# Causal attention with a block FFN: the key tiles of a query block in another order

## The chip, the cores and the metric

The kernel runs on one core of one Trainium2 chip. The metric is the device time of one execution in microseconds (us), lower is better. TensorE (PE) multiplies, VectorE (DVE), ScalarE (ACT) and GpSimd (POOL) do the elementwise work, and SyncE (SP) issues the transfers.

## The reference

Two sequences of 2048 rows with 256 features go through pre-normalised causal attention with 16 heads of 64, a residual and a layer norm, then a gated FFN with a residual and a layer norm:

```python
hn = (h - mu) * rsqrt(var + 1e-05) * gamma + beta
q, k, v = rope(hn @ Wq + bq), rope(hn @ Wk + bk), hn @ Wv + bv      # 16 heads of 64
attn = softmax(where(tril, einsum('bihd,bjhd->bhij', q, k) / 8, -inf))
x = layernorm(h + (einsum('bhij,bjhd->bihd', attn, v) @ Wo + bo + h))
x = layernorm(x + (silu(x @ wg) * (x @ wu)) @ wd)                   # weights are int / 127
```

## The kernel before

After a prologue come 16 iterations, one for each pair of heads and sequence (8 pairs, 2 sequences), and after them the output projection and the FFN. The change lies in the iterations.

**Units.** The 2048 queries are 4 blocks of 512 columns, the keys are 16 tiles of 128. A unit (`UNITS`) is one key tile against one query block, for both heads of the pair. Block b has 4b + 4 key tiles, so an iteration has 4 + 8 + 12 + 16 = 40 units. The last four tiles of a block lie on the diagonal: the unit of tile 4b + i works only on the columns from 128i on, so it is 512, 384, 256 or 128 columns wide, and it has four small matmuls with the mask (L1215) as well. All other units are 512 wide without a mask. I call a unit by its width, with an m where it has the mask: 512, 512m, 384m, 256m, 128m.

**Groups.** Two units in a row are a group; an iteration is 20 groups, g0 to g19. Block 0 is g0 and g1, block 1 g2 to g5, block 2 g6 to g11, block 3 g12 to g19. What PE does in a group is written out by hand, in this order:

1. M1, a piece of the maxima: scores of a later iteration or block in single precision of one part (L1184), written to `m_ps`, of which there is one buffer. DVE reduces it (L833), and no further maxima start before that.
2. S, the scores of the two units into `s_ps` (L1205 to L1215), each behind the exponential of the unit two before.
3. M2, a second piece of maxima (not in g1, g5, g11 and g19, where `M_COUNT` is 1).
4. One use of the bank `x_ps` from the table `XUSE`: T, the turn of the maxima of the next block (L1222, in g1, g5, g11, g19); or X, a piece of the projection of the next pair's q or k, or of v (L1139 to L1141, in g3, g4, g7, g8, g10, g13, g15, g17 for q and k, and g9, g14, g16, g18 for v in most iterations).
5. M3, a third piece, in g3, g8, g13 and g15.
6. W, probabilities times values for the two units of the group before (L1239).
7. R, the row sums of a finished block (L1246), in g0, g2, g6 and g12, behind the last W of that block.

**The other engines.** ACT takes the exponential of each unit (L591) into one of five slots of `pt`. POOL adds the slot into the sums `acc` (L542; the first two units of a block by L537, and in block 0 also L532). R waits until POOL is through with the block. DVE works in its own fixed order: in each group T's input (L847), the transpose of R's result (L882), the rotary products of the X of the group before (L860, L864, which free `x_ps`), the reductions of M1 and M2, the rounding rest of the piece before (L876), the division of a finished block (L887, L890, L895), then the sum with the half that was swapped (L871), which waits for transfers that SP issues behind L860 (`rot<-qr`), and last the reduction of M3.

All this order is static: each engine follows its own list, and semaphores count units, so none of it moves with the key tile that a unit holds.

Of the kernel before, what the change touches and what calls it, by code (L numbers as in the profile page):

```python
# [5 lines left out]
ALU = mybir.AluOpType  # L6
# [7 lines left out]
P = 128  # L14
# [12 lines left out]
BLOCKS = SEQ // NB  # L27
# [4 lines left out]
MASKED = -1e30  # L32


UNITS = [(b, j, max(0, j - 4 * b) * P) for b in range(BLOCKS) for j in range(4 * b + 4)]
NU = len(UNITS)

MUNITS = [(t, c, min(NB, (t + 1) * P - c * NB)) for t in range(TT) for c in range(t // 4 + 1)]
# [14 lines left out]
def units_to(b):  # L53

    return sum(4 * a + 4 for a in range(b))
# [46 lines left out]
def postln_block_kernel(nc, h, gamma, beta, wqkv, bqk, bv, wo, bo, wgate_t, wup_t, wdown_t,  # L102
                        cos, sin, ident, masks, attn, hn_far, v_far, out):
    h, out = h.rearrange("b s d -> (b s) d"), out.rearrange("b s d -> (b s) d")
    with ExitStack() as ctx:
        def sb(name, shape, dt):
            return ctx.enter_context(nc.sbuf_tensor(name, shape, dt))
# [13 lines left out]
        ones_f = sb("ones_f", [P, DK], F32)  # L121
# [20 lines left out]
        with ExitStack() as ctx_attn:  # L142
            def sba(name, shape, dt):
                return ctx_attn.enter_context(nc.sbuf_tensor(name, shape, dt))
# [17 lines left out]
            acc = sba("acc", [P, 2, 2, NB], F32)  # L162
# [144 lines left out]
        FIRST, MIDDLE, SWITCH, LAST = "first", "middle", "switch", "last"  # L307

        def each_pair(engine, pair):

            kinds = {0: FIRST, PAIRS - 1: SWITCH, 2 * PAIRS - 1: LAST}
            for it in range(2 * PAIRS):
                pair(kinds.get(it, MIDDLE), it, it % 2, it % PAIRS, it // PAIRS)
# [3 lines left out]
        def group_units(g):  # L317
            return range(GU * g, GU * g + GU)
# [192 lines left out]
        @block.gpsimd  # L511
        def _(pool):
            pool.wait_ge(primed, 1)

            def next_rows(t):

                nc.gpsimd.tensor_scalar(h_all[1][:, t, :], h_all[1][:, t, :], mv[:, TT + t, 0:1],
                                        rstd[:, TT + t:TT + t + 1], ALU.subtract, ALU.mult).then_inc(next_norm, 1)

            def pair(kind, it, par, pr, batch):  # L520
                for u in range(NU):
                    blk, j, q0 = UNITS[u]
                    if j == 0 and blk > 0:
                        continue
                    pool.wait_ge(exped, it * NU + (u + 1))
                    if j <= 1 and (kind is not FIRST or blk >= 2):
                        pool.wait_ge(r_done, it * BLOCKS + (blk - 1))
                    for a in range(2):
                        sums = acc[:, blk % 2, a, q0:NB]
                        probs = pt[:, u % SLOTS, a, q0:NB]  # L530
                        if j == 0:
                            last = nc.gpsimd.tensor_tensor(acc[:, 0, a, 0:P], probs[:, 0:P],  # L532
                                                           ones_f[:, 0:1].broadcast_to([P, P]), ALU.mult)
                            if a == 1:
                                last.then_inc(summed, 1)
                        elif j == 1:
                            last = nc.gpsimd.tensor_tensor(sums, pt[:, (u - 1) % SLOTS, a, q0:NB], probs, ALU.add)  # L537
                            if a == 1:
                                last.then_inc(summed, 4 if blk > 0 else 3)
                        else:  # L540
                            pool.wait_ge(summed, it * (2 * NU) + (2 * u + a - 1))
                            nc.gpsimd.tensor_tensor(sums, sums, probs, ALU.add).then_inc(summed, 1)  # L542


            pool.wait_ge(a_rstd, len(STAT_TILES))
            for t in range(TT):
                next_rows(t)
            each_pair(pool, pair)

        @block.scalar  # L550
        def _(act):
# [30 lines left out]
            def exp_unit(kind, it, u):  # L582
                blk, j, q0 = UNITS[u]
                if kind is not FIRST or u >= SLOTS:
                    act.wait_ge(pv_done, it * NG + ((u - SLOTS) // GU + 1))
                    act.wait_ge(summed, it * (2 * NU) + 2 * (u - SLOTS + 1))
                if kind is FIRST and u == 0:
                    act.wait_ge(a_turned, 2 * TURNS)
                act.wait_ge(scored, it * NU + (u + 1))
                two = 2 * (u % 2)  # L590
                nc.scalar.activation(pt[:, u % SLOTS, :, q0:NB], s_ps[:, two:two + 2, q0:NB], ACT.Exp, scale=SCALE)\  # L591
                  .then_inc(exped, 1)
# [544 lines left out]
        def _(pe):  # L1137
# [55 lines left out]
            def scores(kind, it, par, u):  # L1193
                blk, j, q0 = UNITS[u]
                if kind is not FIRST or u >= 2:
                    pe.wait_ge(exped, it * NU + (u - 1))
                if j == 0:
                    pe.wait_ge(aux_done, it * BLOCKS + (blk + 1))
                    pe.wait_ge(qk_lo, it * (2 * BLOCKS) + 2 * (blk + 1))
                q, k = slice(NB * blk + q0, NB * (blk + 1)), slice(j * P, (j + 1) * P)  # L1200
                two = 2 * (u % 2)
                dst = [s_ps[:, two + a, q0:NB] for a in range(2)]
                diag = j >= 4 * blk
                for a, rows in enumerate(halves):
                    nc.tensor.matmul(dst[a], qk[par][rows, 1, k], qk[par][rows, 0, q], start=True, stop=False)  # L1205
                for a, rows in enumerate(halves):
                    nc.tensor.matmul(dst[a], qk[par][rows, 1, k], qk[par][rows, 2, q], start=False, stop=False)  # L1207
                for a, rows in enumerate(halves):
                    nc.tensor.matmul(dst[a], qk[par][rows, 3, k], qk[par][rows, 0, q], start=False, stop=False)  # L1209
                for a, rows in enumerate(halves):  # L1210
                    last = nc.tensor.matmul(dst[a], ones_r[rows, :], aux[rows, q0:NB], start=False, stop=not diag)  # L1211
                if diag:
                    for x in range(2):
                        for a, rows in enumerate(halves):
                            last = nc.tensor.matmul(s_ps[:, two + a, q0 + DK * x:q0 + DK * (x + 1)],  # L1215
                                                    mask_b[rows, x, :], id_b[rows, :], start=False, stop=x == 1)
                last.then_inc(scored, 1)
# [7 lines left out]
            def weigh(kind, it, par, g):  # L1225

                for u in group_units(g):
                    blk, j, q0 = UNITS[u]
                    n = 4 * blk + 4
                    pe.wait_ge(exped, it * NU + (u + 1))  # L1230
                    if j == 0:
                        if blk == 0:
                            pe.wait_ge(v_in, 16 * (it + 1))
                        if blk == BLOCKS - 1:
                            pe.wait_ge(v_in3, 16 * (it + 1))
                        if blk > 0 or kind is not FIRST:
                            pe.wait_ge(o_out, it * BLOCKS + blk)
                    for a, rows in enumerate(halves):
                        last = nc.tensor.matmul(o_ps[rows, q0:NB], v[par][:, j, rows], pt[:, u % SLOTS, a, q0:NB],  # L1239
                                                start=(j == 0), stop=(j == n - 1), skip_group_check=True)  # L1240
                last.then_inc(pv_done, 1)

            def sums(it, blk):
# [5 lines left out]
            def pair(kind, it, par, pr, batch):  # L1249
# [30 lines left out]
                for g in range(NG):  # L1280
# [24 lines left out]
                    if g > 0:  # L1305
                        weigh(kind, it, par, g - 1)
                    elif kind is not FIRST:
                        weigh(kind, it - 1, 1 - par, NG - 1)
# [101 lines left out]
            pe.wait_ge(c_lo, OC)  # L1410
            project_out(0, o_first)
            weigh(LAST, FINAL, 1, NG - 1)
            pe.wait_ge(r_turned, FINAL * BLOCKS + 3)
            sums(FINAL, BLOCKS - 1)
# [63 lines left out]
```

## Time and profile before

| | |
|---|---|
| median of 3 runs | 2231.38 us (2230.36 to 2232.55) |
| the profiled execution's own time | 2229.82 us |
| its span in the trace | 2228.0 us |
| PE busy | 2070.0 us, 93% |
| DVE busy | 1597.6 us, 72% |
| POOL busy | 1391.7 us, 62% |
| ACT busy | 906.6 us, 41% |

A share of busy time is an average over the prologue, the iterations and the FFN. The iterations take the time from 72.9 us to about 1880 us. The rows of a timeline give the start and the length of a run of equal instructions, and in brackets the time that the engine stood idle before it and what ended that. Matmuls overlap, so the cost of a step on PE is read from the start of its first matmul to the start of the next step's.

### The profile page before, as it was taken

The page shows a single profiled execution, that of the slowest core. Times are in us where ns is not written, and L with a number is a line of the kernel's source. Part 1 is how long each engine was busy: PE and PEld are TensorE (multiplying, and loading weights), DVE is VectorE, ACT ScalarE, POOL GpSimd, SP SyncE. Part 2 cuts the span into 40 slices and gives each one's busy share as a digit, 9 for nine tenths or more (in the row PEclk, how much of TensorE's full clock was granted, in tenths as well). Part 3 has the DMA queues.
Part 4 walks back from the last instruction along what each step waited for, and adds up shares of the span by engine and source line. Part 5 has one row for each costly group of instructions (what it writes and reads, how often), then busy time and mean ns, then how long its engine had stood idle before and what let it go on. Part 6 is the DMA issues. An engine that isn't in the chain of part 4 may idle for free.

```text
span 2228.0 us, 37497 instructions
## 1 busy us (share of the span) xinstructions
PE 2070.0 (93%) x14720; PEld 1287.2 (58%) x14720; DVE 1597.6 (72%) x2262; ACT 906.6 (41%) x1245; POOL 1391.7 (62%) x1204
## 2 busy tenths in 40 slices
PE   6779999999999989999999999999999989889997
PEld 5445555555555545555555555555555545789996
DVE  8576878686878776767777777778787763556654
ACT  4424443444444434434343434343434345434342
POOL 1457777777787866677767777878787879000000
PEclk9899999999999999999999999999999999999999
DMA  6311212121202122122111212121112131231300
GB/s 223 119 30 38 62 39 62 39 62 39 58 25 68 42 68 72 45 65 63 48 53 43 58 43 58 43 58 34 48 34 58 29 119 48 67 104 57 112 10 29
DMA packets 116149, 132.16 MB, mean 59 GB/s; under 512 B 15248, under 2 KB 71184, under 8 KB 115728
## 3 DMA queue, kind: packets, MB, share of 16 engines
q1 hardware_dynamic: 115984, 129.92, 19.5%
q8 instruction: 109, 1.79, 0.3%
q14 instruction: 56, 0.46, 0.1%
HBM read 56.47 MB, written 39.85 MB: 43 GB/s over the span
## 4 chain that ended last, share of the span: by engine, by line
PE 60%; DVE 24%; DMA 5%; SPq 4%; issue 4%; ACT 1%; POOL 1%; ACTq 0%; DVEq 0%
PE o_ps L1239 13%; DVE mpart L833 9%; PE m_ps L1184 7%; DMA rot<-qr 5%; PE s_ps L1205 4%; SPq L385 4%; PE s_ps L1209 4%; PE s_ps L1207 4%; PE s_ps L1211 4%; PE x_ps L1139 3%; DVE qr L860 3%; PE x_ps L1246 3%; DVE qc L871 2%; PE gu_ps L1139 2%; PE gu_ps L1140 2%
## 5 line engine op out<-in xcount | busy, mean ns | idle before, releaser
L542 POOL TENSOR_TENSOR acc<-acc,pt 128x512 f32<-128x512 f32 (+3 forms) x1024 | 1195.8, 1200 | 228.0 <-ACT pt L591 228.0
L591 ACT ACTIVATE pt<-s_ps 128x1024 f32<-128x1024 f32 (+3 forms) x640 | 544.8, 895 | 704.8 <-PE s_ps L1211 342.4
L833 DVE TENSOR_REDUCE mpart<-m_ps 128x2 f32<-128x1024 f32 (+2 forms) x576 | 624.9, 1085 | 288.2 <-PE m_ps L1184 215.7
L1239 PE MATMUL o_ps<-pt,v 128*64 128x512 f32 (+3 forms) x2560 | 547.5, 549 | 0.0
L1184 PE MATMUL m_ps<-qk 64*128 64x512 f32 (+3 forms) x1280 | 290.0, 449 | 85.0 <-DVE mpart L833 73.7
L1184 PEld LDWEIGHTS m_ps<-qk 64*128 64x128 f32 x1280 | 121.1, 185 | 395.6 <-DVE mpart L833 223.6
L1239 PEld LDWEIGHTS o_ps<-pt,v 128*64 128x64 f32 x2560 | 157.8, 138 | 239.1 <-issue 213.8
L537 POOL TENSOR_TENSOR acc<-pt 128x512 f32<-128x512 f32 (+1 forms) x128 | 161.7, 1283 | 193.7 <-ACT pt L591 193.7
L1205 PE MATMUL s_ps<-qk 64*128 64x512 f32 (+3 forms) x1280 | 253.7, 392 | 0.0
L1209 PE MATMUL s_ps<-qk 64*128 64x512 f32 (+3 forms) x1280 | 235.6, 363 | 0.0
L1211 PE MATMUL s_ps<-aux,ones_r 64*128 64x512 f32 (+3 forms) x1280 | 234.7, 362 | 0.0
L1207 PE MATMUL s_ps<-qk 64*128 64x512 f32 (+3 forms) x1280 | 234.3, 362 | 0.0
L871 DVE TENSOR_TENSOR qc<-qc,rot 128x512 f32<-128x512 f32 x128 | 139.6, 1091 | 113.4 <-DMA rot<-qr 113.3
L569 ACT ACTIVATE qk<-qc 128x512 fp32r<-128x512 f32 x128 | 80.0, 629 | 253.2 <-DVE qc L871 253.2
L876 DVE TENSOR_TENSOR qk<-qc,qk 128x512 fp32r<-128x512 f32 x128 | 140.8, 1103 | 0.2 <-ACT qk L569 0.2
L1209 PEld LDWEIGHTS s_ps<-qk 64*128 64x128 f32 x1280 | 121.2, 185 | 20.3
L1211 PEld LDWEIGHTS s_ps<-aux,ones_r 64*128 64x128 f32 x1280 | 121.5, 185 | 19.1
L1207 PEld LDWEIGHTS s_ps<-qk 64*128 64x128 f32 x1280 | 122.1, 187 | 16.5
L1205 PEld LDWEIGHTS s_ps<-qk 64*128 64x128 f32 x1280 | 122.1, 187 | 15.8 <-ACT pt L591 4.9
L1139 PE MATMUL x_ps<-hn,w_hl 128*128 128x512 f32 x240 | 107.7, 449 | 0.0
L1141 PE MATMUL x_ps<-hn,w_hl 128*128 128x512 f32 x240 | 95.3, 397 | 0.0
L1140 PE MATMUL x_ps<-hn,w_hl 128*128 128x512 f32 x240 | 95.1, 396 | 0.0
(165 smaller groups left out, 2882.0 us busy)
## 6 DMA issues: line engine op xcount, KB each, us to landing
rot<-qr SPq DMA_DIRECT2D x512, 64.0 KB, 2.0
attn<-o_sum SPq DMA_DIRECT2D x64, 256.0 KB, 2.3
o_raw<-attn SPq DMA_DIRECT2D x8, 2048.0 KB, 8.9
v<-v_far SPq DMA_DIRECT2D x16, 768.0 KB, 5.2
v_far<-v_part SPq DMA_DIRECT2D x48, 256.0 KB, 2.0
w_raw<-in_wqkv SPq DMA_DIRECT2D x34, 128.0 KB, 5.1
v_far<-v SPq DMA_DIRECT2D x16, 256.0 KB, 2.4
v<-v_far SPq DMA_DIRECT2D x16, 256.0 KB, 5.0
```

The source lines that it names most:

```text
L537: last = nc.gpsimd.tensor_tensor(sums, pt[:, (u - 1) % SLOTS, a, q0:NB], probs, ALU.add)
L542: nc.gpsimd.tensor_tensor(sums, sums, probs, ALU.add).then_inc(summed, 1)
L591: nc.scalar.activation(pt[:, u % SLOTS, :, q0:NB], s_ps[:, two:two + 2, q0:NB], ACT.Exp, scale=SCALE)\
L833: nc.vector.tensor_reduce(dst, m_ps[:, :, 0:w], AX.X, ALU.max, negate=True).then_inc(maxed, 1)
L871: nc.vector.tensor_tensor(qc[:, c % 2, a, :], qc[:, c % 2, a, :], rot[:, a, :], ALU.add).then_inc(roped, 1)
L1139: nc.tensor.matmul(dst, lhs[0], rhs[0], start=first, stop=False)
L1184: last = nc.tensor.matmul(m_ps[:, a, 0:w], qk[par][rows, 0, q], qk[par][rows, 1, k], start=True, stop=not diag)
L1205: nc.tensor.matmul(dst[a], qk[par][rows, 1, k], qk[par][rows, 0, q], start=True, stop=False)
L1207: nc.tensor.matmul(dst[a], qk[par][rows, 1, k], qk[par][rows, 2, q], start=False, stop=False)
L1209: nc.tensor.matmul(dst[a], qk[par][rows, 3, k], qk[par][rows, 0, q], start=False, stop=False)
L1211: last = nc.tensor.matmul(dst[a], ones_r[rows, :], aux[rows, q0:NB], start=False, stop=not diag)
L1239: last = nc.tensor.matmul(o_ps[rows, q0:NB], v[par][:, j, rows], pt[:, u % SLOTS, a, q0:NB], start=(j == 0), stop=(j == n - 1), skip_group ...
```

## The change

The key tiles of a block come in an order given by a table. Tile 0 stays first. The two units of a group are now:

| block | groups before | groups after |
|---|---|---|
| 0 | g0 512m 384m, g1 256m 128m | g0 512m 256m, g1 384m 128m |
| 1 | g2, g3 whole, g4 512m 384m, g5 256m 128m | g2 whole, g3 512m 384m, g4 512 256m, g5 512 128m |
| 2 | g6 to g9 whole, g10 512m 384m, g11 256m 128m | g6 whole, g7 512 256m, g8 whole, g9 512m 384m, g10 whole, g11 512 128m |
| 3 | g12 to g17 whole, g18 512m 384m, g19 256m 128m | g12, g13 whole, g14 512 256m, g15, g16 whole, g17 512m 384m, g18 whole, g19 512 128m |

(whole: 512 and 512.) What each group does besides its two units is as before, and so are all waits, which count units. The last matmul of a block's W is marked by the table, and POOL's first two additions of a block by their place and not by the tile. In block 0 the second unit is 256 wide in place of 384, so POOL's copy (L532) is 256 wide in place of 128 and the addition behind it 256 in place of 384.

```diff
-UNITS = [(b, j, max(0, j - 4 * b) * P) for b in range(BLOCKS) for j in range(4 * b + 4)]
+KEY_TILES = [[0, 2, 1, 3],
...
+             [0, 1, 2, 3, 4, 14, 5, 6, 7, 8, 12, 13, 9, 10, 11, 15]]
+UNITS = [(b, j, max(0, j - 4 * b) * P) for b in range(BLOCKS) for j in KEY_TILES[b]]
...
                 for u in range(NU):
                     blk, j, q0 = UNITS[u]
-                    if j == 0 and blk > 0:
+                    n = u - units_to(blk)
+                    if n == 0 and blk > 0:
                         continue
                     pool.wait_ge(exped, it * NU + (u + 1))
-                    if j <= 1 and (kind is not FIRST or blk >= 2):
+                    if n <= 1 and (kind is not FIRST or blk >= 2):
                         pool.wait_ge(r_done, it * BLOCKS + (blk - 1))
...
-                        if j == 0:
-                            last = nc.gpsimd.tensor_tensor(acc[:, 0, a, 0:P], probs[:, 0:P],
-                                                           ones_f[:, 0:1].broadcast_to([P, P]), ALU.mult)
+                        if n == 0:
+                            alone = UNITS[u + 1][2]
+                            last = nc.gpsimd.tensor_tensor(acc[:, 0, a, 0:alone], probs[:, 0:alone],
+                                                           ones_f[:, 0:1].broadcast_to([P, alone]), ALU.mult)
...
-                        elif j == 1:
+                        elif n == 1:
...
-                                                start=(j == 0), stop=(j == n - 1), skip_group_check=True)
+                                                start=(j == 0), stop=(j == KEY_TILES[blk][-1]), skip_group_check=True)
```

On PE, from the second scores of g4 to the W of g5 in an iteration of the middle, the rows before are these (`m_ps` is M, `s_ps` is S, `x_ps<-id_f,mz` is T, `o_ps` is W):

```order
L1205 MATMUL s_ps<-qk 128x384 [waits exped]
L1211 MATMUL s_ps<-aux,ones_r 128x384 x2
L1184 MATMUL m_ps<-qk 128x128 [waits maxed]
L1184 MATMUL m_ps<-qk 128x512 [waits maxed]
L1205 MATMUL s_ps<-qk 128x256 [waits exped]
L1205 MATMUL s_ps<-qk 128x128 [waits exped]
L1222 MATMUL x_ps<-id_f,mz 128x128 [waits mz_done,cos_done]
L1239 MATMUL o_ps<-pt,v 64x512 [waits exped]
L1239 MATMUL o_ps<-pt,v 64x384 [waits exped]
```

In the same place on PE the changed kernel, whose lines stand seven later, has these:

```order
L1212 MATMUL s_ps<-qk 128x256 [waits exped]
L1218 MATMUL s_ps<-aux,ones_r 128x256 x2
L1191 MATMUL m_ps<-qk 128x128 [waits maxed]
L1191 MATMUL m_ps<-qk 128x512 [waits maxed]
L1212 MATMUL s_ps<-qk 128x512 [waits exped]
L1212 MATMUL s_ps<-qk 128x128 [waits exped]
L1229 MATMUL x_ps<-id_f,mz 128x128 [waits mz_done,cos_done]
L1245 MATMUL o_ps<-pt,v 64x512 [waits exped]
L1245 MATMUL o_ps<-pt,v 64x256 [waits exped]
```

Columns moved from the scores of g4, in front of M2, to those of g5, in front of T; the waits stand where they stood.

On POOL, the end of block 3 and the start of the next iteration's block 0 before:

```order
L542 TENSOR_TENSOR acc<-acc,pt 128x384 [waits summed,exped]
L542 TENSOR_TENSOR acc<-acc,pt 128x384 [waits summed]
L542 TENSOR_TENSOR acc<-acc,pt 128x256 [waits summed,exped]
L542 TENSOR_TENSOR acc<-acc,pt 128x256 [waits summed]
L542 TENSOR_TENSOR acc<-acc,pt 128x128 [waits summed,exped]
L542 TENSOR_TENSOR acc<-acc,pt 128x128 [waits summed]
L532 TENSOR_TENSOR acc<-pt,ones_f 128x128 [waits r_done,exped]
L532 TENSOR_TENSOR acc<-pt,ones_f 128x128
L537 TENSOR_TENSOR acc<-pt 128x384 [waits r_done,exped]
L537 TENSOR_TENSOR acc<-pt 128x384
```

In the same place on POOL in the changed kernel:

```order
L549 TENSOR_TENSOR acc<-acc,pt 128x512 [waits summed,exped]
L549 TENSOR_TENSOR acc<-acc,pt 128x512 [waits summed]
L549 TENSOR_TENSOR acc<-acc,pt 128x128 [waits summed,exped]
L549 TENSOR_TENSOR acc<-acc,pt 128x128 [waits summed]
L539 TENSOR_TENSOR acc<-pt,ones_f 128x256 [waits r_done,exped]
L539 TENSOR_TENSOR acc<-pt,ones_f 128x256
L544 TENSOR_TENSOR acc<-pt 128x256 [waits r_done,exped]
L544 TENSOR_TENSOR acc<-pt 128x256
```

The last group of the block now ends with 640 columns of additions for each head where it had 384, and three whole units stand ahead of the last one.

## Rows read from the trace of the kernel before

**Rows 1.** The page: span, and PE's busy time, share and instructions.

```profile
span 2228.0 us, 37497 instructions
PE 2070.0 (93%) x14720; PEld 1287.2 (58%) x14720; DVE 1597.6 (72%) x2262; ACT 906.6 (41%) x1245; POOL 1391.7 (62%) x1204
```

**Rows 2.** The page: the chain that ended last, shares by engine.

```profile
PE 60%; DVE 24%; DMA 5%; SPq 4%; issue 4%; ACT 1%; POOL 1%; ACTq 0%; DVEq 0%
```

**Rows 3.** Waits, whole run: us in total, times, longest.

```profile
PEld m_ps L1184 <- DVE mpart L833: 223.6, 270, 3.5
DVE qc L871 <- DMA rot<-qr: 113.3, 82, 4.6
```

**Rows 4.** PE timeline, iteration 4, g2: its scores, then M2.

```profile
561.79 0.40 PE L1205 MATMUL s_ps<-qk 64*128 64x512 f32 x2
...
563.64 0.40 PE L1184 MATMUL m_ps<-qk 64*128 64x512 f32 x2
```

**Rows 5.** PE timeline, iteration 4: M1 of g4 to M2 of g6.

```profile
572.71 0.50 PE L1184 MATMUL m_ps<-qk 64*128 64x512 f32 x2 [0.43 <-DVE mpart L833]
...
577.06 1.94 PE L1239 MATMUL o_ps<-pt,v 128*64 128x512 f32 x8
578.92 0.50 PE L1184 MATMUL m_ps<-qk 64*128 64x512 f32 x2
...
581.71 0.66 PE L1222 MATMUL x_ps<-id_f,mz 128*128 128x128 f32 x4 [1.17 <-DVE qc L864]
582.29 1.73 PE L1239 MATMUL o_ps<-pt,v 128*64 128x512 f32 x8
583.95 0.50 PE L1184 MATMUL m_ps<-qk 64*128 64x512 f32 x2
...
586.72 0.49 PE L1184 MATMUL m_ps<-qk 64*128 64x512 f32 x2 [0.41 <-DVE mpart L833]
```

**Rows 6.** PE timeline, iteration 4: M2 of g10.

```profile
610.33 0.50 PE L1184 MATMUL m_ps<-qk 64*128 64x512 f32 x2 [1.31 <-DVE mpart L833]
```

**Rows 7.** DVE timeline, iteration 4, g6.

```profile
584.84 0.69 DVE L871 TENSOR_TENSOR qc<-qc,rot 128x512 f32<-128x512 f32 x1 [1.28 <-DMA rot<-qr]
...
588.40 1.52 DVE L876 TENSOR_TENSOR qk<-qc,qk 128x512 fp32r<-128x512 f32 x1
```

**Rows 8.** PE timeline, iteration 5: scores, M2, W, R of g0; g1 to T.

```profile
659.84 0.39 PE L1205 MATMUL s_ps<-qk 64*128 64x512 f32 x2
...
660.84 0.42 PE L1205 MATMUL s_ps<-qk 64*128 64x384 f32 x2
...
661.69 0.50 PE L1184 MATMUL m_ps<-qk 64*128 64x512 f32 x2
662.11 0.87 PE L1239 MATMUL o_ps<-pt,v 128*64 128x256 f32 x8
662.82 1.03 PE L1246 MATMUL x_ps<-acc,ones_f 128*64 128x512 f32 x4
...
664.12 0.36 PE L1205 MATMUL s_ps<-qk 64*128 64x256 f32 x2
...
664.75 0.30 PE L1205 MATMUL s_ps<-qk 64*128 64x128 f32 x2
...
665.39 0.66 PE L1222 MATMUL x_ps<-id_f,mz 128*128 128x128 f32 x4
```

**Rows 9.** POOL timeline, iteration 4: start of block 2; last 16 additions of block 3.

```profile
588.10 2.99 POOL L537 TENSOR_TENSOR acc<-pt 128x512 f32<-128x512 f32 x2 [5.09 <-ACT pt L591]
...
643.22 18.37 POOL L542 TENSOR_TENSOR acc<-acc,pt 128x512 f32<-128x512 f32 x16 [0.53 <-ACT pt L591]
```

**Rows 10.** POOL's groups with shapes apart: busy us, mean ns.

```profile
L542 POOL TENSOR_TENSOR acc<-acc,pt 128x512 f32<-128x512 f32 x672 | 923.1, 1404 | 192.1 <-ACT pt L591 192.1
...
L542 POOL TENSOR_TENSOR acc<-acc,pt 128x256 f32<-128x256 f32 x128 | 97.7, 784 | 35.9 <-ACT pt L591 35.9
```

**Rows 11.** One line of DVE, L871: ns minimum, median, maximum.

```profile
L871 DVE TENSOR_TENSOR qc<-qc,rot x128: 671/876/1820, 30.0 to 1781.4; 128x512 f32<-128x512 f32 x128
```

More of the change, by code:

```diff
@@ L1228, in weigh @@
                     blk, j, q0 = UNITS[u]
-                    n = 4 * blk + 4
                     pe.wait_ge(exped, it * NU + (u + 1))
```

2 rows, old and new, of the table KEY_TILES are left out of this document.

## Prediction

> **What bounds the kernel now.** I read the page first: PE is busy for 93% of 2228.0 us [rows 1]. That leaves at most 7% for any change of order, and the order neither adds nor removes work on PE. Next comes the chain that ended last: only 60% of it is PE; 24% is DVE, and 9% is transfers and SP's issuing of them [rows 2]. So PE is nearly full, and still DVE sets the pace in places. The waits say where: weight loads of the maxima waited 223.6 us for the reduction of the piece before, and DVE's own sum L871 waited 113.3 us for the swapped halves [rows 3]. Last I read the timeline of one undisturbed iteration, number 4 (553.4 to 659.6 us), group by group, and looked for the places where PE stands in front of a wait. I call such a place a gate: PE comes before DVE is ready, so the time of the gate is DVE's, whatever PE did just before. There are gates at M1 of g4 (0.43 us), at T of g5 (1.17 us), at M2 of g6 (0.41 us) [rows 5] and M2 of g10 (1.31 us) [rows 6], and smaller ones in g4, g8, g9, g11, g12, g14, g16 and g17. From g18 to the M1 of the next g4, and in two short stretches behind g10 and g15, PE doesn't wait, and PE's work is the time.
>
> **What each unit costs on PE.** From the first matmul of a step to that of the next: two whole units take 563.64 - 561.79 = 1.85 us, 0.93 each [rows 4]. In g0 the 512m takes 1.00 and the 384m 0.85; in g1 the 256m 0.63 and the 128m 0.64 [rows 8]. W of two whole units takes 578.92 - 577.06 = 1.86 us, of 512 and 384 columns 583.95 - 582.29 = 1.66 [rows 5], of 256 and 128 columns 0.71 [rows 8]. That is 0.23 us for each 128 columns or a little less, so I put 512 and 128 at 1.17, 512 and 256 at 1.40, 384 and 128 at 0.94. No row shows these mixed pairs. For scores their cost lies between the sum by columns and the sum of the two units as measured, 0.1 us apart; I take the measured units.
>
> **The change group by group.** Scores: a group that was 512m 384m (1.85) and becomes 512 256m (about 1.53) loses 0.32; so do g7 and g14, which were whole. A group that was 256m 128m (about 1.24) and becomes 512 128m (1.57) gains 0.33: g5, g11, g19. Block 0 moves 0.25 from g0 to g1. W follows a group later: +0.46 in g0, g6 and g12 (1.17 for 0.71), +0.20 in g11 and g19, +0.23 in g2; -0.26 in g1 and g5, -0.20 in g4, g10 and g18, -0.46 in g8 and g15. The sums are zero within the error, as they must be.
>
> What counts is on which side of a gate each piece lies. Taken away in front of a gate it saves nothing, since PE then waits longer; put behind a gate, where PE leads, it costs its full price.
> - g18 to the M1 of g4, PE leads: W18 -0.20, S19 +0.33, W19 +0.20, S0 -0.25, W0 +0.46, S1 +0.25, W1 -0.26, W2 +0.23. Sum +0.76.
> - g4 to T of g5: -0.32 in S4, -0.20 in W4, +0.33 in S5. PE reaches T about 0.2 earlier against DVE, T stays where DVE puts it: 0. M2 of g6 likewise, with W5 -0.26 in front of it: 0.
> - Behind M2 of g6: W6 +0.46 puts R off. The transpose that reads R stands on DVE behind an L876 that begins at 588.40 and takes 1.52 us [rows 7], so R is covered there. PE's own scores of g7 then end 0.46 - 0.32 later: +0.14.
> - g7 to g11: -0.46 in W8 and -0.20 in W10 lie before gates. S11 +0.33 and W11 +0.20 are taken up by the waits left at T of g11 and M2 of g12: 0.
> - Behind M2 of g12: W12 +0.46, R as much later, and no L876 covers it here. +0.46.
> - g13 to g17: S14 -0.32 is before a gate; of W15 -0.46 about 0.20 is saved until the reduction of g15's third maxima is the later. -0.20.
>
> Together +1.16 us for an iteration. 13 of the 16 have this shape (1 to 5 and 8 to 14, and I count half each of 6 and 7): about 15 us. Iteration 0 waits for its larger maxima until g10 and has only the end of the pattern, 6 and 7 have the other halves, and in the last, where POOL sets the pace at the end, its 1.2 us less work ahead of the last units comes back: +2 us for these together.
>
> **DVE and POOL in each other's way.** L871 takes 0.671 us at the least and 1.820 at the most [rows 11]. On the gate of g6 it took 0.69 because POOL stood idle then: its next addition began at 588.10 after 5.09 us of idleness [rows 7, 9]. After the change g5 and g11 hold a whole unit, whose two additions take 1.4 us each where those of the 256m took 0.78 [rows 10], so POOL is still at work when L871 of g6 and g12 comes, and both lie on the path. Bounds: 0 if it misses them, 2 x (1.82 - 0.69) = 2.3 us an iteration if it is held fully both times. By my sum of POOL's times only the tail with the 128-wide additions overlaps, so I stay near the low end: 0.6, which is 8 us over 13 iterations. The Trainium skill (SBUF — State Buffer, on the shared port pair) says that a DVE instruction with two SBUF inputs and a GpSimd instruction that reads SBUF exclude each other for a whole instruction, and the one issued second waits. The spread from 671 to 1820 ns agrees with that; by a wait of half a 1.4 us addition each time the term would be 1.4 us and not 0.6.
>
> **POOL's end of a block.** R of g0 waits for POOL. In iteration 4 POOL's last 16 additions of block 3 run from 643.22 for 18.37 us, to 661.59 [rows 9], and R starts at 662.82 [rows 8], 1.23 us later. Two 512-wide additions now stand there for two 256-wide: 2 x (1.404 - 0.784) = 1.24 us more [rows 10], while R comes W18 to W0, 0.54 us, later. About 0.5 us of margin is left, so I count 0; without it each 0.1 us costs 0.1. At the other blocks POOL is through well before R in the timeline, and the wider copy in block 0 falls into its idle time. ACT has the same exponentials, 41% busy: 0. DMAs are the same and wait for the same events: 0.
>
> **Sum.** 15 + 2 + 8 = 25 us, against the profiled execution's own 2229.8 us: 2255. The median of the runs is 1.6 us above that, so for a median I say 2256, 1.1% slower.
>
> **Rivals.** (a) No change that can be measured (a measurement of this kernel tells about 0.2%, 4 to 5 us, from nothing): if every shift that I put on PE's path is covered as that of R in g6 is. For it: all three transitions W0, W6, W12 are followed by DVE work. Against: in g0 to g3 PE has no wait at all. Time 2231. Chance 0.12.
> (b) Faster. Behind g4, g10 and g18 the waits at T of g5 (1.17 us) and g11 exist because those groups are short on PE. If work taken away in front of a gate lets DVE start its chain sooner, since DVE too waits for PE's maxima in many groups, the added 0.33 at S5 and 0.33 + 0.20 at S11 and W11 fill waits for nothing: 0.86 us an iteration, 11 us, 2220. It decides if DVE's chain from M2 of g4 to T of g5 starts with PE and not with its own backlog. Against: M1 of g4 already waits for DVE [rows 5]. Chance 0.13.
> (c) Slower by more, through POOL: the margin at R of g0 is gone and L871 is held most of the time. The price is 1.16 + 1.7 + 1.0 = 3.9 us an iteration, 50 us: 2281. It sets in once POOL ends block 3 more than 0.5 us later than I have it. For it: POOL runs without a gap for 18 us there. Chance 0.17.
> My forecast, about 2240 to 2268, has 0.58.
>
> **Range.** 2228 to 2278: it leaves out half of (b) and half of (c). Faster by over 0.2%: 0.13, (b). Within: 0.12, (a). Slower: 0.75.
>
> **What the profile after would show.** Right: T of g5 and M2 of g6 wait at least as long as before, against 1.17 and 0.41 us; M1 of g9 behind the shorter W8 waits more; R of g12 and all behind it comes about 0.46 later; L871 of g6 and g12 takes over 0.69 us; PE's idle time grows by some 1 to 2 us in each iteration, its busy time stays. Wrong: if the gates of g5 and g6 come closer to g4's M2, DVE wasn't bound by its own list but by PE (b). If R of g0 shows a wait for POOL, (c) is at work. Most of all the forecast would fail if PE's path from g18 to g4 has room that the rows don't show, since two thirds of the sum come from there.

## The result: 0.26% slower, a fifth of what was forecast

| | median us | runs |
|---|---|---|
| before | 2231.51 | 22 |
| changed | 2236.58 | 22 |

The ratio is 1.0026, with a 95% interval from 1.0016 to 1.0036: 5 us slower, where 25 us were forecast. The direction is right and the size is not. One execution of a kernel below (only_b1, 6629 us) lies far outside all others and stands in no number here.

The page of the changed kernel: the span, the engines, and the shares of the chain that ended last. Against [rows 1, 2], PE's busy time is 3.5 us less while the span is 4.7 us more.

```profile
span 2232.7 us, 37497 instructions
...
PE 2066.5 (93%) x14720; PEld 1294.1 (58%) x14720; DVE 1619.9 (73%) x2262; ACT 902.9 (40%) x1245; POOL 1402.0 (63%) x1204
...
PE 62%; DVE 24%; DMA 5%; issue 4%; SPq 4%; ACT 1%; POOL 0%; ACTq 0%; DVEq 0%
```

The waits of the whole run, which answer to [rows 3] (total, times, longest). The first hardly moved and the second fell by 10 us, while the kernel became slower, so the totals can't tell where 5 us went.

```profile
PEld m_ps L1191 <- DVE mpart L840: 223.1, 286, 3.2
...
DVE qc L878 <- DMA rot<-qr: 102.9, 87, 4.5
```

PE's timeline in iteration 4 from W of g0 to R of g0 and W of g1, then from M1 of g4 to R of g6. The second part answers to [rows 5].

```profile
556.75 1.30 PE L1245 MATMUL o_ps<-pt,v 128*64 128x512 f32 x8
557.88 1.03 PE L1252 MATMUL x_ps<-acc,ones_f 128*64 128x512 f32 x4
...
561.27 1.51 PE L1245 MATMUL o_ps<-pt,v 128*64 128x512 f32 x8
562.71 0.49 PE L1191 MATMUL m_ps<-qk 64*128 64x512 f32 x2
...
574.37 0.51 PE L1191 MATMUL m_ps<-qk 64*128 64x512 f32 x2 [0.47 <-DVE mpart L840]
576.82 0.33 PE L1191 MATMUL m_ps<-qk 64*128 64x128 f32 x2 [0.45 <-DVE mpart L840]
...
582.21 0.66 PE L1229 MATMUL x_ps<-id_f,mz 128*128 128x128 f32 x4
...
587.75 0.50 PE L1191 MATMUL m_ps<-qk 64*128 64x512 f32 x2 [1.15 <-DVE mpart L840]
```

The prices of the mixed pairs were right: W of 512 and 128 takes 557.88 - 556.75 = 1.13 us (forecast 1.17), of 512 and 256 562.71 - 561.27 = 1.44 (1.40). But the reader should look at T. In iteration 4, before, it came 581.71 - 572.71 = 9.00 us after M1 of g4, behind a wait of 1.17 us [rows 5]. Now it comes after 582.21 - 574.37 = 7.84 us and no wait stands in front of it. M2 of g6 comes 13.38 us after M1 of g4 instead of 14.01. The gates had come nearer. Iteration 4, on which the forecast was built, shows this larger than most. In the twelve iterations of this shape T came nearer to the start of g4 by 0.36 us in the mean, by 1.17 in iteration 4 and by 0.20 to 0.23 in eight of them. Before the change T waited 1.17 to 1.19 us in three of the twelve (3, 4 and 10), and 0.21 to 0.24 us in eight.

### The profile page after: what moved, and what is told of

It reads as the page before. It is cut to its first block, busy times and chain, and to the rows that moved or that the text cites. A ratio compares the mean times of both kernels' runs of the same rounds, so it can differ in the third digit from the quotient of the medians.

```text
span 2232.7 us, 37497 instructions
## 1 busy us (share of the span) xinstructions
PE 2066.5 (93%) x14720; PEld 1294.1 (58%) x14720; DVE 1619.9 (73%) x2262; ACT 902.9 (40%) x1245; POOL 1402.0 (63%) x1204
## 4 chain that ended last, share of the span: by engine, by line
PE 62%; DVE 24%; DMA 5%; issue 4%; SPq 4%; ACT 1%; POOL 0%; ACTq 0%; DVEq 0%
PE o_ps L1245 14%; DVE mpart L840 9%; PE m_ps L1191 8%; PE s_ps L1212 4%; DMA rot<-qr 4%; PE s_ps L1216 4%; PE s_ps L1214 4%; PE s_ps L1218 4%; SPq L390 4%; PE x_ps L1146 3%; DVE qr L867 3%; PE x_ps L1252 2%; DVE qc L878 2%; PE gu_ps L1146 2%; PE gu_ps L1147 2%
## 5 line engine op out<-in xcount | busy, mean ns | idle before, releaser
L549 POOL TENSOR_TENSOR acc<-acc,pt 128x512 f32<-128x512 f32 (+3 forms) x1024 | 1208.9, 1213 | 311.6 <-ACT pt L598 311.6
L544 POOL TENSOR_TENSOR acc<-pt 128x512 f32<-128x512 f32 (+1 forms) x128 | 152.6, 1214 | 121.0 <-ACT pt L598 121.0
L878 DVE TENSOR_TENSOR qc<-qc,rot 128x512 f32<-128x512 f32 x128 | 141.9, 1109 | 102.9 <-DMA rot<-qr 102.9
L883 DVE TENSOR_TENSOR qk<-qc,qk 128x512 fp32r<-128x512 f32 x128 | 152.1, 1191 | 0.0
L1214 PEld LDWEIGHTS s_ps<-qk 64*128 64x128 f32 x1280 | 121.9, 187 | 18.5
```

The source lines that it names most:

```text
L878: nc.vector.tensor_tensor(qc[:, c % 2, a, :], qc[:, c % 2, a, :], rot[:, a, :], ALU.add).then_inc(roped, 1)
```

## The experiments

All ratios are to the kernel before. A difference between two experiments is a difference of their ratios times 2231 us, rough to some 4 to 8 us, since each interval is 0.3 to 0.6% wide. To follow the time inside an iteration I took, from the trace of each kernel, the time from the first scores of an iteration to each place (the row of L1205 or of M), as a mean over the 12 iterations 1 to 5 and 8 to 14, and subtracted two kernels. That table stands below the experiments.

**One block at a time.** Each kernel has one row of the table in the new order and natural order in the others, for block 2:

```diff
...
-             [0, 1, 4, 5, 2, 6, 3, 7],
+             [0, 1, 2, 3, 4, 5, 6, 7],
              [0, 1, 2, 10, 3, 4, 8, 9, 5, 6, 7, 11],
...
```

> Only block 0 has the new order; the other blocks have their tiles in natural order. The theory of gates (DVE's chain fixes T of g5, M2 of g6, g10 and g12; only PE work between gates costs): S0 -0.25, S1 +0.25, W1 -0.26, W2 +0.23, so within 1 us of before. Rival, that the shifts of the other blocks matter little and the cost comes from POOL's wider copy and its holding of the port in g0 and g1: 3 us or more slower.

> Only block 1 has the new order. Theory of gates with an easier port: the copy in front of T of g5 is 0.3 us shorter, L871 of g6 is 0.5 us longer, the W of g6 is covered by L876: 0 to 3 us slower in all. Rival (my forecast's own terms): T of g5 does not move, L871 of g6 is held, +0.46 of W6 partly on the path: 6 us or more slower. Rival (b): the longer g5 fills the wait at T for nothing: 3 us or more faster.

> Only block 2 has the new order. Theory of gates: M2 of g12 stays, the W of g12 behind it is 0.46 us longer and not covered: +0.46 for 15 iterations, 5 to 7 us slower. Rival: the gates of g8 to g12 come earlier since g7 and g8 are shorter (-0.32 and -0.46) and cancel it: within 2 us of before.

> Only block 3 has the new order. Theory of gates: between g18 and the next g4 PE leads, so W18 -0.20, S19 +0.33, W19 +0.20, W0 +0.46 count in full, and about -0.2 to -0.4 is saved at W15: +0.4 to +0.6 an iteration, 6 to 9 us slower. Rival: what g0 to g3 are put off by is regained at the gates of g5 and g6, so within 2 us of before.

| run | ratio | 95% interval |
|---|---|---|
| only_b0 | 1.0005 | 0.9990 to 1.0021 |
| only_b1 | 0.9997 | 0.9982 to 1.0012 |
| only_b2 | 1.0022 | 1.0008 to 1.0036 |
| only_b3 | 1.0024 | 1.0009 to 1.0040 |

Blocks 0 and 1 cost nothing that can be measured, 2 and 3 some 5 us each: what the theory of gates gave for block 2, a little under what it gave for block 3. The intervals for blocks 2 and 3 leave out zero, but with their lower ends at 2 us they touch the rivals' "within 2 us". In the traces M2 of g6 comes 0.31 us earlier with only block 1 changed, and with only block 2 changed everything from g13 on comes 0.51 us later, behind the W of g12, as expected.

**The same program again.** `none` is the changed code with the table in natural order.

> The changed kernel's code with the table in natural order, so the same instructions as before. Every theory: within 0.1% of before. Its trace shows what differs between two executions of one program: if transfers of the swapped halves are late by 1.5 us in other iterations than in the trace of before, then such lateness is chance and no effect of the order; if in the same ones, it belongs to the program.

Ratio 0.9996 (0.9978 to 1.0015). Its trace has the late transfers in the same iterations 2, 9, 12 and 13 (the first is 0). Here is why they are late. DVE's timeline of the kernel before, iteration 2, first L860 of the second piece and then the L871 that waits for its halves:

```profile
353.75 0.74 DVE L860 SCALAR_TENSOR_TENSOR qr<-x_ps,b_qk,sin_sb 128x512 f32<-128x512 f32 x1
...
359.78 0.69 DVE L871 TENSOR_TENSOR qc<-qc,rot 128x512 f32<-128x512 f32 x1 [2.61 <-DMA rot<-qr]
```

From the end of L860 to L871 are 5.29 us; in most iterations they are 3.85. The transfers of the same stretch by queue (packets, MB, share of the engines):

```profile
q1 hardware_dynamic: 192, 0.26, 19.8%
q8 instruction: 1, 0.02, 1.3%
```

Between the same two instructions of iteration 3, 4.0 us there, queue 8 is absent:

```profile
q1 hardware_dynamic: 192, 0.26, 27.1%
```

One packet of the instruction queue, 16 KB, sits on one transfer engine for 1.3% of 16 engines' 5.5 us, 1.1 us. In iterations 2, 9, 12 and 13 it begins 3.0 to 3.6 us after L860, three last packets of the swapped half move only when it has ended, and L871 comes 5.3 to 5.6 us after L860. In the changed kernel the same packets begin 3.5 to 3.6 us after L860, all pieces of the halves have moved by then, and L871 comes after 3.84 us. In `none` they begin after 1.6 to 3.7 us and L871 comes after 4.7 to 5.8. So this belongs to the program, as a meeting in time. The start of the packet alone doesn't decide it: 3.55 us was late in the kernel before, 3.46 to 3.60 was not in the changed one; which engine the packet sat on the traces don't say. With the short copy these four iterations are free of it in old_reduce and new_reduce. Iteration 14 has a packet that begins earlier, 0.5 us after L860 before and 0.6 in the changed kernel, and is late in both (4.80 and 4.83 us).

**The small copy.** L847 copies 8 elements for each partition. Its row in the kernel before and, as L854, in the changed one (ns minimum, median, maximum):

```profile
L847 DVE COPY mz<-mc x64: 166/968/1253, 55.7 to 1848.0; 128x8 f32<-128x8 f32 x64
```

```profile
L854 DVE COPY mz<-mc x64: 159/883/1259, 56.2 to 1852.7; 128x8 f32<-128x8 f32 x64
```

A copy of 0.16 us takes six times as long in the middle, beside POOL. In g5 of iteration 4 it ends 0.03 to 0.04 us behind an addition of POOL, 384 wide before and 256 wide after. The edit writes it as a reduction over one element, in the old and in the changed order:

```diff
-                nc.vector.tensor_copy(mz[:, :, :].rearrange("p t (a d) -> p t a d", a=2)[:, :, :, 0], mc[:, blk, :, :])\
+                nc.vector.tensor_reduce(mz[:, :, :].rearrange("p t (a d) -> p t a d", a=2)[:, :, :, 0],
+                                        mc[:, blk, :, :].unsqueeze(3), AX.X, ALU.max)\
```

> Order of before; the small copy L847 (8 elements for each partition, 0.6 to 1.25 us beside POOL) is written as a reduction over one element. Theory that the copy waits for the port that it shares with POOL, and that it lies on the path at T of g5: it takes under 0.3 us, M2 of g6 comes up to 0.7 us earlier in an iteration, 5 to 12 us faster in all. Rival, that the length of the copy has another reason (the strided write): it stays at 0.6 us or more, within 2 us of before. Rival, that it shortens but T then waits for something else: within 3 us.

> The changed order, with the copy written as a reduction too. If the changed order gained back part of its price by a shorter copy at T of g5 (0.70 for 0.97 us), then that gain is gone where the copy is short in both: the distance to the old order with the same reduction is 0.3 us an iteration more than between the two kernels as they were, 8 to 10 us in place of 5. Rival: the distance stays at 5 us or falls.

| run | median us | ratio | 95% interval |
|---|---|---|---|
| old_reduce | 2203.92 | 0.9870 | 0.9843 to 0.9898 |
| new_reduce | 2219.74 | 0.9953 | 0.9928 to 0.9978 |

The row of the reduction in old_reduce:

```profile
L854 DVE TENSOR_REDUCE mz<-mc x64: 152/154/170, 55.6 to 1818.6; 128x8 f32<-128x8 f32 x64
```

It is 0.15 us throughout, and the old order is 27 us faster, over twice what I expected. Between the two orders there are now 16 us by the medians and 19 by the ratios, not 5. So the first expectation was right in kind and too small, and of the second even the larger number was too small: the copy hid most of the price of the new order.

**POOL out of the way.** The additions take 16 columns, so these two kernels leave out part of the row sums and serve for their times alone:

```diff
-                            nc.gpsimd.tensor_tensor(sums, sums, probs, ALU.add).then_inc(summed, 1)
+                            nc.gpsimd.tensor_tensor(sums[:, 0:16], sums[:, 0:16], probs[:, 0:16], ALU.add).then_inc(summed, 1)
```

> Order of before, the small copy as a reduction, and POOL's additions from the third unit of a block on take only 16 columns for each head, so that part of the row sums is left out; the waits are as they were. POOL no longer holds the shared port nor is it late at a block's end. L871 and L876 of DVE take 0.7 us each throughout. Both theories: faster than old_reduce, by 10 us or more, as DVE's chains to M2 of g8, g10 and g12 shorten.

> The changed order with the same reduction and the same 16 columns. What is left between this and old_thin is PE's work on this or that side of a gate. Theory of gates: 1.16 us an iteration as forecast, 12 to 18 us. Rival, that most of the 16 us between the two orders with the reduction is DVE held by POOL at L871 of g6 and g12: 8 us or less. Rival, that without POOL's hold PE leads nearly everywhere, so that it no longer matters where its work lies: 5 us or less.

old_thin: 2144.66 us, ratio 0.9615 (0.9599 to 0.9631). new_thin: 2157.24 us, 0.9673 (0.9656 to 0.9691). The distance is 13 us, inside the 12 to 18 of the theory of gates; both rivals fall. DVE's sum, here L879, in old_thin, which answers to [rows 11]:

```profile
L879 DVE TENSOR_TENSOR qc<-qc,rot x128: 677/692/980, 30.2 to 1702.9; 128x512 f32<-128x512 f32 x128
```

In old_reduce, from which only POOL's width differs, its median is 968 ns and its maximum 1808; here they are 692 and 980: POOL was the reason for the spread. The old order gains 59 us over old_reduce.

**Which part of the order costs.** Both have the reduction and natural order in block 0. keep_ends and wide_ends:

```diff
-KEY_TILES = [[0, 1, 2, 3], [0, 1, 4, 5, 2, 3, 6, 7], [0, 1, 2, 3, 4, 5, 8, 9, 6, 7, 10, 11],
-             [0, 1, 2, 3, 4, 5, 6, 7, 8, 9, 12, 13, 10, 11, 14, 15]]
+KEY_TILES = [[0, 1, 2, 3], [0, 1, 2, 6, 4, 5, 3, 7], [0, 1, 2, 3, 4, 5, 6, 10, 8, 9, 7, 11],
+             [0, 1, 2, 3, 4, 5, 6, 7, 8, 9, 10, 14, 12, 13, 11, 15]]
```

> Small copy as a reduction; the 512m 384m group of blocks 1 to 3 comes one to two groups earlier, and the last group of each block stays 256m 128m. If what costs is the work behind the last gates of a block (W of g0, g6, g12, scores of g19), this order costs nothing: within 3 us of old_reduce (ratio about 0.987 of before). Rival, that any order in which masked units leave the end costs: 8 us or more slower than old_reduce.

> Small copy as a reduction; 512m 384m stays one group in its place, and in blocks 1 to 3 only the 256m changes place with a whole unit, so that the last group is 512 128m (block 3: g17 512 256m, g19 512 128m). Theory of gates: S19 +0.33, W0 +0.46, W12 +0.46 count, W18 -0.46 and S3 -0.32 are saved: about +0.5 us an iteration, 6 to 10 us slower than old_reduce. Rival, that the whole changed order's 16 us comes from the wide last groups alone: 14 us or more.

keep_ends: 2199.18 us, ratio 0.9865 (0.9844 to 0.9885), as old_reduce. Masked units can leave the end of a block for nothing that these runs can measure, if the last group stays narrow. wide_ends: 2213.36 us, 0.9923 (0.9903 to 0.9943), 12 us above old_reduce by the ratios and 9 by the medians: around the upper end of the 6 to 10 expected, and less than the rival's 14. The 256m alone, changed for a whole unit in the last group, makes about 60 to 70% of the whole price (12 of 19 us by the ratios, 1.09 of 1.54 us an iteration in the traces).

**The theory used forward, and a miss.** Natural order but for block 1, `[0, 1, 6, 2, 3, 4, 5, 7]`, with the reduction:

> Small copy as a reduction, natural order but in block 1, which is 0, 1, 6, 2, 3, 4, 5, 7: the 256m comes to g3. Theory of gates used forward: S3 -0.32 in front of M2 of g3, where PE leads, is saved; W4 -0.46, S4 +0.08, W5 +0.20, S5 +0.25 lie in front of gates and count nothing; W6 +0.23 is covered by L876 of g6. But L871 of g6 may be held longer, since POOL has a 384m where it had a 256m: up to +0.2. In sum 0 to 4 us faster than old_reduce, ratio 0.985 to 0.987 of before. Rival, that a heavier last group always costs its full W and scores: 0.23 + 0.25 - 0.32 = +0.2 an iteration, 3 us slower.

2208.24 us, ratio 0.9911 (0.9890 to 0.9932), 9 us above old_reduce by the ratios, 4 by the medians. M1 of g4 comes 0.42 us later in the mean instead of 0.3 earlier: 0.63 to 0.66 later in ten iterations, 0.65 to 0.68 earlier in iterations 2 and 10. The cause stands in the trace. DVE's division (L903) and the reduction behind it in g3 of iteration 4 of early_256:

```profile
564.26 1.81 DVE L903 TENSOR_TENSOR o_sum<-o_sum,r_t 128x512 f32<-128x512 f32 x1
565.99 1.21 DVE L840 TENSOR_REDUCE mpart<-m_ps 128x2 f32<-128x1024 f32 x1
```

The same in old_reduce:

```profile
564.36 0.94 DVE L903 TENSOR_TENSOR o_sum<-o_sum,r_t 128x512 f32<-128x512 f32 x1
565.22 1.21 DVE L840 TENSOR_REDUCE mpart<-m_ps 128x2 f32<-128x1024 f32 x1
```

PE was ahead as I had worked out and DVE issued the division 0.1 us earlier than in old_reduce. But the narrower unit on POOL put the next whole addition 0.01 us ahead of the division, which then stood through all of it: 1.81 us for 0.94. A saving of 0.30 us at M2 of g3 turned into a loss of 0.64 at M1 of g4. The two iterations that gained are the test: in 2 and 10 POOL's addition begins 0.20 and 0.22 us behind the division, which takes 0.79 and 0.80 us; in the ten others the two begin within 0.03 us of each other and it takes 1.80 to 1.82.

**Inside an iteration.** Later (+) or earlier (-) than the old order of the same kind, in us, counted from the iteration's first scores:

| place | forecast | changed - before | new_reduce - old_reduce | new_thin - old_thin |
|---|---|---|---|---|
| start of g4 | +0.43 | +0.63 | +0.64 | +0.52 |
| M2 of g6 | +0.43 and part of 0.6 for the port | +0.19 | +1.01 | +0.49 |
| start of g8 | +0.57 | +0.08 | +1.01 | +0.48 |
| start of g13 | +1.03 | +0.47 | +1.42 | +0.92 |
| start of g16 | +0.83 | +0.05 | +0.99 | +0.47 |
| end | +1.16, with the port 1.76 | +0.48 | +1.54 | +1.01 |

How far such a mean can be trusted is seen from `none` less before, two executions of one program: at these places it is between -0.14 and +0.19 us, and single iterations differ by up to 3.5 us.

**The granted clock.** One cause of such differences is TensorE's clock. PE's rows in iteration 9 around M2 of g6, before:

```profile
1162.79 0.80 PE L1184 MATMUL m_ps<-qk 64*128 64x512 f32 x2 [2.13 <-DVE mpart L833]
1163.52 1.55 PE L1239 MATMUL o_ps<-pt,v 128*64 128x256 f32 x8
1164.85 1.67 PE L1246 MATMUL x_ps<-acc,ones_f 128*64 128x512 f32 x4
```

The same in `none`:

```profile
1164.08 0.50 PE L1191 MATMUL m_ps<-qk 64*128 64x512 f32 x2 [1.28 <-DVE mpart L840]
1164.52 0.87 PE L1245 MATMUL o_ps<-pt,v 128*64 128x256 f32 x8
1165.22 1.03 PE L1252 MATMUL x_ps<-acc,ones_f 128*64 128x512 f32 x4
```

The busy time of each engine in the same stretch of the kernel before (us and instructions), the granted clock, and DMA:

```profile
1162.70:1166.10 3.40, 3.31 (x14) 1.48 (x14) 2.39 (x3) 1.99 (x3) 1.93 (x2) 0.50 0.00 0
```

PE had stood idle for 2.13 us in the kernel before, and from 1162.7 to 1166.1 us the granted clock was 0.50, the lower of its two levels (1.2 and 2.4 GHz). In `none` it had waited 1.28 us and the clock was 1.00. The slow stretch of 3.4 us put off M1 of g7 by another 1.6 us. Not every long wait was followed by one: those of 2.15 and 2.03 us at the same place in iterations 12 and 13 were not.

The mean granted clock was 0.979 in the trace of before and 0.982 in the changed one, which is 94 and 80 us at the lower level. Of the twelve iterations of the table, before has such a stretch in 2 and 9 and the changed kernel in none; those two came out 1.66 and 1.23 us faster after the change, and the other ten 0.87 us slower in the mean, not 0.48 (+0.35 at the start of g8, +0.44 at g16). Both of the two met the packet as well, as did 12 and 13, which came out 0.43 and 0.06 us faster. The four kernels of the two right columns have no such stretch in the twelve. Over whole executions it is the same: the median clock is 0.981 in the 22 of the changed kernel and 0.978 in the 76 of the kernel before that ran beside the experiments. Those at 0.980 took 2227.0 us before (mean of 8) and 2237.9 changed (5), those at 0.979 2228.6 (21) and 2239.8 (3). So among executions with the same mean clock the new order is about 11 us slower, and some half of that is missing in the medians, where the changed kernel has the higher clock. No run tried the clock by itself.

## Why the forecast failed

**Where it was right.** PE leads from g18 to g4, and the work moved there costs its price: +0.63 by g4 (forecast +0.43), and +0.21 from g18 to the end (forecast +0.33). W of g12 costs 0.42 and 0.43 in the two right columns, for 0.46 (0.27 in the first, where iteration 2 of the kernel before ran this place at the lower clock). With POOL out of the way, 1.01 us an iteration were measured for 1.16 forecast, and 13 us for 15. With POOL but the short copy, 1.54 for 1.76. That T waits no longer was in the forecast the sign of rival (b), by which the work in the short groups fills waits for nothing. It wasn't (b) as written: the kernel became slower, and DVE's own instructions took less time, as shown below. Rival (c) stood at its threshold and no further. PE's R of g0 in iteration 5 and POOL's additions in front of it:

```profile
664.40 1.08 PE L1252 MATMUL x_ps<-acc,ones_f 128*64 128x512 f32 x4
```

```profile
655.05 9.20 POOL L549 TENSOR_TENSOR acc<-acc,pt 128x512 f32<-128x512 f32 x8 [0.36 <-ACT pt L598]
```

POOL is done at 664.25 and R starts 0.15 us later, where 1.23 us lay before [rows 8, 9]: nearly all of the margin has gone, as against 0.5 us left by my sum. But R waits for nothing: from W to R are 1.13 us here as in every other iteration. And the margin is so small in 5 of 15 iterations only; in the others R starts 1.7 us or more behind POOL.

**The step that failed** is the second one, "PE reaches T about 0.2 earlier against DVE, T stays where DVE puts it: 0. M2 of g6 likewise". I took the time of DVE's own list from the trace as a constant, and one iteration for all. It isn't a constant: from the start of g4 to M2 of g6 it became 0.44 us shorter in the mean, against 0 in the forecast and a part of the port's 0.6. Besides, all prices of PE were taken at one clock, and the granted clock rose (above). The rows of DVE in iteration 4 of the kernel before:

```profile
577.96 1.48 DVE L871 TENSOR_TENSOR qc<-qc,rot 128x512 f32<-128x512 f32 x1 [1.74 <-DMA rot<-qr]
579.37 0.98 DVE L847 COPY mz<-mc 128x8 f32<-128x8 f32 x1
```

The same two in the changed kernel, and the L878 and L883 of g6, which answer to [rows 7]:

```profile
578.89 1.21 DVE L878 TENSOR_TENSOR qc<-qc,rot 128x512 f32<-128x512 f32 x1 [1.01 <-DMA rot<-qr]
580.02 0.70 DVE L854 COPY mz<-mc 128x8 f32<-128x8 f32 x1
...
585.22 1.34 DVE L878 TENSOR_TENSOR qc<-qc,rot 128x512 f32<-128x512 f32 x1 [0.36 <-DMA rot<-qr]
...
589.43 1.51 DVE L883 TENSOR_TENSOR qk<-qc,qk 128x512 fp32r<-128x512 f32 x1
```

Between M1 of g4 and M2 of g6, in means over the 12 iterations:
- the copy's end comes 0.32 us sooner behind L871, where POOL has 256-wide additions and not 384;
- L871 itself is 0.08 shorter and its first wait 0.06;
- L871 of g6 starts 0.44 sooner behind its L860, since in four iterations the halves no longer meet the instruction packet. In iteration 5 it starts 1.3 us later, though the halves come on time: the two DVE instructions in front of it, L883 and L859, take 1.78 and 1.77 us where L876 and L852 took 0.97 and 0.94;
- L871 of g6 is 0.46 longer, held by the whole unit of g5, as forecast.

Spread over the iterations, the four with the packet make nearly all of it: M2 of g6 comes 1.0 to 1.4 us nearer to M1 of g4 there, and in the mean of the eight others by 0.02 us, where hold and relief cancel.

With the copy's share and the packets' gone in both orders, and no slow clock in the twelve, as in the kernels with the reduction, what was forecast comes to light: +1.54 an iteration for 1.76. old_reduce and new_reduce take away the copy's share and the packets' together, and the clock's with them in the twelve iterations. So they show that these together hid the price; how it divides among them was only read from the traces. The two traced executions with the reduction lie 9.9 us apart, not 18.5 (12 x 1.54): new_reduce is 8.6 us faster in the rest of the program, with a granted clock of 0.984 for 0.979.

**The port's term was one-sided.** I gave it 0.6 us, between 0 and 2.3, and looked only at the two L871 that would be held anew. These came out as forecast, +0.46 at g6 and +0.15 at g12 (0.69 to 0.84 us), 0.61 together. But each instruction of DVE that shares the port with POOL may also be freed, and I excluded that without a reason: the copy (-0.32), the L871 in front of it (-0.08) and L871 of g8 (1.63 to 1.26 us in the mean) give more than that back. The Trainium skill (SBUF — State Buffer, on the shared port pair) names copies in a two-port mode among the instructions that take the pair, beside those with two SBUF inputs; the copy's 0.16 to 1.26 us next to 0.15 us for the reduction agree with that. It also says that reductions on trn2 never contend; the reduction in place of the copy, 0.152 to 0.170 us in all 64 cases, agrees. And its rule that the second to be issued waits for the whole instruction agrees with early_256, 1.81 us for 0.94.

**Smaller sizes.** g7: the forecast had +0.14 between M2 of g6 and g8, measured -0.11 (0.00 in the ten iterations without a slow stretch). W15 saved 0.42 and not 0.20. The iterations of other shapes, +2 us in the forecast, came out 1.5 us faster, by -0.3, +1.2, -2.7 and +0.4 us for 0, 6, 7 and the last; number 7 has a stretch of 3.4 us at the lower clock before and none after, and between before and `none` it differs by 2.7 us, with 3.4 and 10.2 us at that clock. The 12 iterations give 12 x 0.48 = 5.8 us.

**What stays open.** Whether the sum over single blocks (0.48%, with four intervals of 0.15% each way, so some 0.3%) is really more than the whole change (0.26%). In the traces of the whole, most of what g0 to g4 lost is regained by M2 of g8 (+0.63 to +0.24), and so it is with block 3 alone (+0.44 to +0.07). The single kernels too differ in their clock, by medians of 0.977 to 0.980. I tried no pair of blocks.

## What to carry to other kernels

A gate, where one engine waits for another's list, hides what is moved in front of it, up to the length of its wait, and what is moved behind it, where the engine leads, cost its full price here; so keep the work narrow behind the last gate and not even across groups. Read the length of a gate from all iterations: T's 1.17 us stood in three of twelve. But before taking the list's length as fixed, look at minimum, median and maximum of each of its instructions: the ones with a wide spread hung on a third engine here, and the change moved that one too. Compare the granted clock of the two kernels before giving a difference of 0.3% to the order. And an instruction of 8 elements that takes 1 us deserves a try in another form, before any order is tuned around it: here that was worth 1.3%, five times what the change of order cost.

## What the runs showed of the hardware

- A copy of 8 elements for each partition on DVE, SBUF to SBUF, took 0.16 us at the least and 0.97 in the median beside POOL's additions; as a reduction over one element it took 0.15 to 0.17 us in all 64 cases. Writing 64 of them as reductions saved 27 us.
- One packet of the instruction queue (16 KB, about 1.1 us on one transfer engine) held the end of a small SBUF transfer back by 0.9 to 1.9 us, in the same four iterations in two executions of one program (before and `none`).
- A division on DVE took 1.80 to 1.82 us where an addition of POOL began within 0.03 us of it, and 0.79 and 0.80 us where it began 0.20 and 0.22 us later (early_256).
- A stretch of 3.4 us at a granted clock of 0.50, behind a wait of PE of 2.13 us, put PE off by 1.6 us against another execution of the same program. Executions of the kernel before ranged from 2221 to 2240 us with mean clocks from 0.983 to 0.973.
